# Cutting the feed-forward of an early-fusion layer into nine token tiles of 488 instead of eight batches of 548

## The chip, the cores and the metric

One core of a Trainium2 chip runs the whole kernel. TensorE (PE; its weight loads are PEld), VectorE (DVE), ScalarE (ACT) and GpSimd (POOL) compute; SyncE (SP) issues every DMA here. The metric is the time of one execution on the device, in microseconds (us), as the median over several runs. A profile is one execution, recorded instruction by instruction.

## The reference

Eight batches of 548 tokens (36 image patches, 512 text tokens) with 192 features pass through one layer. Only the last part is changed by this edit, the sum over 16 experts of a gelu network:

```python
h = h + attention(layernorm(h))            # h: (8, 548, 192)
xt = layernorm(h).reshape(-1, 192)         # 4384 tokens
comb = top8_softmax_weights(xt @ router_w.T)       # (4384, 16)
for e in range(16):                        # widths 8 x 128 and 8 x 256, 3072 in all
    hid = gelu(xt @ w1[:, off:off + wd])
    out = out + comb[:, e:e+1] * (hid @ w2[off:off + wd, :])
h = h + out
```

## The kernel before

**Phase A** runs attention, the second layer norm and the router, batch by batch. For each batch SP stores two things in DRAM: the normed input `x2` (three rows of 548 numbers for each of 128 partitions) and the weights `comb` (16 rows of 548). The sum `h` stays in SBUF, with 128 tokens to a partition block: `h[:, b, I, :]`. Phase A ends in a barrier of all engines (`end_of_phase_a`). SP reaches it only after `x2` of the last batch has landed in DRAM (line 236, waiting for `x2_stored`).

**The feed-forward** (lines 1031 to 1065 on DVE, 1085, 1441 and 1442 on PE) has the tokens as columns. For each batch it goes through 24 width tiles k of 128 rows of w1. Experts 0 to 7 have one tile each, experts 8 to 15 have two. Numbers are kept as a high and a low part, so each product costs several matmuls:

- `up(b, k)`: five matmuls for each half of 274 tokens, into two PSUM banks. Two pairs of banks alternate.
- ACT `gelu` writes `act`, DVE `weigh` multiplies it by `gate` (the row of `comb` for the expert, broadcast to 128 partitions), ACT `act_round` writes `act_hi`, DVE `act_rest` (line 795) writes `act_lo`.
- `down(b, k)`: five matmuls for each half, added up in banks 4 to 7 over all k.

PE issues `up(k + 2)` ahead of `down(k)`. On DVE `weigh(k + 1)` stands ahead of `act_rest(k)`, on ACT `gelu(k + 1)` ahead of `act_round(k)`. At the end of a batch ACT and DVE copy the sums out (`out_a`, `out_r`), PE transposes them back to tokens on partitions (ten transposes), DVE adds `h` (`h`, `out_t`), and SP stores the result. The next batch needs the same four banks, so its first `down` waits for that addition.

**What sets the order on SP.** Each engine works its own list in order. SP's list in the feed-forward is the loads of `gate` (four buffers; the load for expert e waits until expert e - 4 has been weighed), the stores of the output, and at one place the loads of `x2` for the last three batches. Those wait until POOL has split the rest of w2 (`w2_split`), since w2 is staged in the memory that they fill. Each load of `x2` also waits for the one before it to land. While SP waits at one instruction, nothing behind it is issued.

Of the kernel before, what the change touches and what calls it, by code (L numbers as in the profile page):

```python
# [31 lines left out]
P = 128  # L32
B = 8
# [31 lines left out]
CREDIT = 1  # L65

# [15 lines left out]
def early_fusion(nc, patches, txt, tok_w, tok_b, gammas, gn_w, gn_b, attn_w, w1, w2, out):  # L82
# [9 lines left out]
    with ctx:  # L92
# [75 lines left out]
        sb("x2_first", [P, B - 3, 3, L], F32, w2_staging)  # L168
        w2_others = sb("w2_others", [P, NW - W2_PART, 256], F32, w2_staging)
        w2_staging.close()  # L170
        x2_all = sb("x2_all", [P, B, 3, L], F32R)
        gate = [sb(f"gate{i}", [P, 2, HALF]) for i in range(4)]
        act = [sb(f"act{i}", [P, 2, HALF]) for i in range(3)]
        act_hi = [sb(f"act_hi{i}", [P, 2, HALF], F32R) for i in range(3)]
        act_lo = [sb(f"act_lo{i}", [P, 2, HALF], F32R) for i in range(3)]
        w2_hi, w2_lo = sb("w2_hi", [P, NW, P], F32R), sb("w2_lo", [P, NW, P], F32R)
        w2_r = sb("w2_r", [P, NW, P], F32R)
        out_a, out_r, out_t = sb("out_a", [P, L]), sb("out_r", [P, L]), sb("out_t", [P, NT, HD])
# [39 lines left out]
        outt_done, out_ready, out_stored = sem("outt_done"), sem("out_ready"), sem("out_stored")  # L218
# [25 lines left out]
        def _(sp):  # L244
# [27 lines left out]
            def store_x2(u, src):  # L272
                sp.wait_ge(x2_lo, nth(u, 3, 3))
                sp.dma_start(x2_dram[bass.ds(u, 1), :, :].rearrange("a p n -> p (a n)"),
                             src[:, :, :].rearrange("p c n -> p (c n)").bitcast(F32)).then_inc(x2_stored, 16)

            def store_ct(u):
                sp.wait_ge(ct_copied, CREDIT + nth(u, 1, 1))
                sp.dma_start(comb_dram[bass.ds(u, 1), :, :].rearrange("a e n -> e (a n)"),
                             ct[:, :]).then_inc(ct_stored, 16)  # L280

            def load_x2(b):
                if b:
                    sp.wait_ge(ld_x2, 16 * b)
                sp.dma_start(x2_all[:, b, :, :].bitcast(F32), x2_dram[b].rearrange("p (c n) -> p c n", c=3)).then_inc(ld_x2, 16)

            def body(b, tail, router, more):
                sp.wait_ge(w1_split, nth(b, 1, 1))
                if more:
                    sp.dma_start(w1_raw, w1[:, :, bass.ds((b + 1) * W1_SHARE, W1_SHARE)]).then_inc(ld_w1, 16)  # L290
                else:
                    sp.dma_start(w2_first, w2[:, 0:W2_PART, :]).then_inc(ld_w2, 16)
                if router:
                    store_x2(b - 2, x2)
                    store_ct(b - 2)

# [11 lines left out]
            for e in range(4):  # L308
                sp.dma_start(gate[e][:, :, :].rearrange("p a n -> p (a n)"),
                             comb_dram[0, e, :].partition_broadcast(P)).then_inc(ld_gate[e], 16)  # L310
            for b in range(2, B - 3):
# [8 lines left out]
            def gates(b, first, end=E):  # L320
                for e in range(first, end):

                    last = LAST_OF[(e - 4) % E] + 1
                    sp.wait_ge(gated, nth(b, NW, last) if e >= 4 else nth(b - 1, NW, last))
                    src = comb_dram[bass.ds(b, 1), e, :].rearrange("a n -> (a n)").partition_broadcast(P)
                    sp.dma_start(gate[e % 4][:, :, :].rearrange("p a n -> p (a n)"), src).then_inc(ld_gate[e % 4], 16)

            def store_out(b):
                sp.wait_ge(out_ready, nth(b, 2, 2))
                dst = out[bass.ds(b, 1), :, :].rearrange("a n d -> (a n) d")  # L330
                src = h[:, bass.ds(b, 1), :, :].rearrange("p a t d -> p (a t) d")
                sp.dma_start(dst[0:(NT - 1) * P, :].rearrange("(t p) d -> p t d", p=P), src[:, 0:NT - 1, :]).then_inc(out_stored, 16)
                sp.dma_start(dst[(NT - 1) * P:L, :], src[0:LAST, NT - 1, :]).then_inc(out_stored, 16)
# [11 lines left out]
            sp.wait_ge(out_stored, 32 * B)  # L345

# [108 lines left out]
        def _(sc_eng):  # L455
# [221 lines left out]
            def gelu(b, k):  # L677
                a.wait_ge(up_done, nth(b, NW, k + 1))
                if k >= 3 or not isinstance(b, int) or b:
                    a.wait_ge(act_lo_ready, nth(b, NW, k - 2))  # L680
                a.activation(act[k % 3][:, :, :], ps[:, 2 * (k % 2):2 * (k % 2) + 2, 0:HALF],  # L681
                             ACT.Gelu_apprx_tanh).then_inc(gelu_done, 1)

            def act_round(b, k):
                a.wait_ge(gated, nth(b, NW, k + 1))
                if k >= 3 or not isinstance(b, int) or b:
                    a.wait_ge(down_done, nth(b, NW, k - 2))
                copy(act_hi[k % 3][:, :, :], act[k % 3][:, :, :]).then_inc(act_hi_ready, 1)

            def ffn(b, more):  # L690

                gelu(b, 2)
                for k in range(2, NW - 1):
                    gelu(b, k + 1)
                    act_round(b, k)
                if more:
                    gelu(b + 1, 0)
                act_round(b, NW - 1)
                if more:
                    act_round(b + 1, 0)  # L700
                    gelu(b + 1, 1)
                a.wait_ge(down_done, nth(b, NW, NW))
                copy(out_a[:, :].rearrange("p (a n) -> p a n", a=2), ps[:, 4:6, 0:HALF]).then_inc(acc_a_copied, 1)
                if more:
                    act_round(b + 1, 1)

            gelu(0, 0)
            gelu(0, 1)
            round_w2(0, W2_HEAD)
            act_round(0, 0)  # L710
            act_round(0, 1)
            round_w2(W2_HEAD, W2_PART)
            ffn(0, True)
            with a.Fori(1, B - 1) as b:
                ffn(b, True)
            ffn(B - 1, False)


        @block.vector
        def _(dve):  # L720
# [306 lines left out]
            def weigh(b, k):  # L1027
                e = TILE_E[k]
                dve.wait_ge(gelu_done, nth(b, NW, k + 1))
                dve.wait_ge(ld_gate[e % 4], 16 * (b * (E // 4) + e // 4 + 1))  # L1030
                dve.tensor_tensor(act[k % 3][:, :, :], act[k % 3][:, :, :], gate[e % 4][:, :, :],  # L1031
                                  ALU.mult).then_inc(gated, 1)

            def act_rest(b, k):
                dve.wait_ge(act_hi_ready, nth(b, NW, k + 1))
                sub(act_lo[k % 3][:, :, :], act[k % 3][:, :, :], act_hi[k % 3][:, :, :]).then_inc(act_lo_ready, 1)

            def ffn(b, more):
                weigh(b, 2)
                for k in range(2, NW - 1):  # L1040
                    weigh(b, k + 1)
                    act_rest(b, k)
                if more:
                    weigh(b + 1, 0)
                act_rest(b, NW - 1)
                if more:
                    act_rest(b + 1, 0)
                dve.wait_ge(down_done, nth(b, NW, NW))
                dve.tensor_copy(out_r[:, :].rearrange("p (a n) -> p a n", a=2), ps[:, 6:8, 0:HALF]).then_inc(acc_r_copied, 1)  # L1049
                if more:  # L1050
                    weigh(b + 1, 1)
                dve.wait_ge(outt_done, nth(b, 1, 1))
                groups = []
                for r, t0, n, bank in ((P, 0, NT - 1, 4), (LAST, NT - 1, 1, 5)):
                    hb = h[:r, bass.ds(b, 1), t0:t0 + n, :].rearrange("p a t d -> p (a t) d")
                    main = ps[:r, bank, 0:P * n].rearrange("p (t d) -> p t d", t=n)
                    rest = ps[:r, bank + 2, 0:P * n].rearrange("p (t d) -> p t d", t=n)
                    groups.append((hb, rest, out_t[:r, t0:t0 + n, :]))
                    last = dve.tensor_tensor(hb[:, :, 0:P], main, hb[:, :, 0:P], ALU.add)
                last.then_inc(out_ready, 1)  # L1060
                for hb, rest, part in groups:
                    dve.tensor_tensor(part, rest[:, :, HD:P], hb[:, :, P:D], ALU.add)
                dve.drain()
                for hb, rest, part in groups:
# [438 lines left out]
```

## Time and profile before

| | |
|---|---|
| median of 3 runs | 899.78 us (898.18 to 900.14) |
| span of the profiled execution | 894.0 us, mean granted TensorE clock 0.969 |
| PE busy | 834.3 us, 93% of the span |
| DVE busy | 574.6 us, 64% |
| ACT busy | 495.9 us, 55% |
| POOL busy | 88.6 us, 10% |
| feed-forward | from the barrier at 377.9 us to the end |

The span runs from the first to the last instruction; what the runs add lies around it. A group of matmuls shows a mean duration that is longer than the distance between two starts, since they overlap; for the rate of a stream the starts are to be read.

### The profile page before, as it was taken

What the parts mean: (1) busy time and instruction counts of PE and PEld (TensorE: products, weight loads), DVE (VectorE), ACT (ScalarE), POOL (GpSimd) and SP (SyncE); (2) the same over time, 40 slices, a digit from 0 to 9 for tenths busy, and PEclk for the clock granted to TensorE, in tenths of its full rate; (3) what the DMA queues carried; (4) which work ended last, traced back from release to release, by engine and by line L of the source; (5) the groups of instructions that cost most, each with busy time, mean ns of one, the idle gap of its engine ahead of it and who ended that gap; (6) DMA issues with size and microseconds to landing.
All of it is one profiled execution on the core that took longest, in us unless ns stands there. A gap on an engine that the chain in (4) does not pass through costs nothing.

```text
span 894.0 us, 18035 instructions
## 1 busy us (share of the span) xinstructions
PE 834.3 (93%) x6048; PEld 764.7 (86%) x6048; DVE 574.6 (64%) x1574; ACT 495.9 (55%) x1102; POOL 88.6 (10%) x162
## 2 busy tenths in 40 slices
PE   5879999999999995779999999999999999999996
PEld 2757878797787874579999999999999999999996
DVE  6657788888888774685565555655655655655554
ACT  1467787887787785434444444444444444444443
POOL 3111131220203021160000000000000000000000
PEclk9789999999999997779999999999999999999999
DMA  8300010101101027422532232232322322322320
GB/s 237 118 19 18 1 57 2 55 2 57 50 7 55 2 75 271 155 76 64 172 104 73 64 95 75 63 90 80 75 75 81 88 63 78 103 71 63 94 65 20
DMA packets 34421, 67.30 MB, mean 75 GB/s; under 512 B 3632, under 2 KB 14160, under 8 KB 34256
## 3 DMA queue, kind: packets, MB, share of 16 engines
q1 hardware_dynamic: 34384, 66.84, 25.3%
q8 instruction: 20, 0.33, 0.1%
q14 instruction: 17, 0.14, 0.1%
HBM read 55.41 MB, written 11.42 MB: 75 GB/s over the span
## 4 chain that ended last, share of the span: by engine, by line
PE 73%; issue 14%; DVE 6%; POOL 2%; ACT 2%; POOLq 2%; DVEq 0%; PEldq 0%; ACTq 0%; PEld 0%
PE ps L1085 67%; PE ps L1224 3%; DVE sc L841 1%; ACT xn L472 1%; PE ps L1124 1%; DVE pr L864 1%; DVE x L795 1%; POOLq L379 1%; POOL w_lo L402 1%; DVE out_r L1049 1%; PE ps L1441 1%; PE ps L1442 0%; PE ps L1303 0%; DVE den L856 0%; DVE w_lo L795 0%
## 5 line engine op out<-in xcount | busy, mean ns | idle before, releaser
L1031 DVE TENSOR_TENSOR act<-act,gate 128x548 f32<-128x548 f32 x192 | 141.0, 738 | 202.8 <-ACT act L681 202.8
L681 ACT ACTIVATE act<-ps 128x548 f32<-128x548 f32 x192 | 120.5, 628 | 247.9 <-PE ps L1085 245.6
L1085 PE MATMUL ps<-x_all,w_hi 128*128 (+1 forms) x1152 | 252.9, 292 | 0.9 <-ACT act L681 0.9
L1085 PE MATMUL ps<-x_all,w_lo 128*128 (+1 forms) x768 | 216.4, 290 | 0.0
L1085 PEld LDWEIGHTS ps<-x_all,w_hi 128*128 128x128 f32 x1152 | 195.0, 190 | 1.2 <-PEq L236 1.0
L1085 PEld LDWEIGHTS ps<-x_all,w_lo 128*128 128x128 f32 x768 | 146.1, 190 | 0.0
L795 DVE TENSOR_TENSOR act_lo<-act,act_hi 128x548 fp32r<-128x548 f32 x192 | 141.6, 738 | 1.3
L459 ACT ACTIVATE act_hi<-act 128x548 fp32r<-128x548 f32 x192 | 125.7, 655 | 19.4 <-DVE act L1031 19.4
L1085 PE MATMUL ps<-act_hi,w_hi 128*128 128x274 f32 x384 | 112.7, 294 | 6.7 <-DVE act_lo L795 4.1
L1085 PE MATMUL ps<-act_lo,w_hi 128*128 128x274 f32 x384 | 111.6, 291 | 0.0
L1085 PE MATMUL ps<-act_hi,w_lo 128*128 128x274 f32 x384 | 111.6, 291 | 0.0
L1085 PE MATMUL ps<-act_lo,w_r 128*128 128x274 f32 x384 | 105.5, 291 | 0.0
L1085 PE MATMUL ps<-act_hi,w_r 128*128 128x274 f32 x384 | 105.1, 291 | 0.0
L1085 PE MATMUL ps<-pt,v 68*128 68x512 f32 (+5 forms) x288 | 82.9, 438 | 0.0
L1085 PEld LDWEIGHTS ps<-act_hi,w_hi 128*128 128x128 f32 x384 | 72.9, 190 | 7.6 <-DVE act_lo L795 4.6
L1085 PEld LDWEIGHTS ps<-pt,v 128*128 128x128 f32 (+1 forms) x288 | 49.3, 192 | 31.1 <-issue 21.7
L1085 PEld LDWEIGHTS ps<-act_hi,w_lo 128*128 128x128 f32 x384 | 73.3, 191 | 0.0
L1085 PEld LDWEIGHTS ps<-act_hi,w_r 128*128 128x128 f32 x384 | 73.2, 191 | 0.0
L1085 PEld LDWEIGHTS ps<-act_lo,w_hi 128*128 128x128 f32 x384 | 73.0, 190 | 0.0
L1085 PEld LDWEIGHTS ps<-act_lo,w_r 128*128 128x128 f32 x384 | 72.9, 190 | 0.0
L524 ACT ACTIVATE pr<-sc,nm 128x580 f32<-128x580 f32 (+4 forms) x120 | 67.2, 564 | 2.7 <-DVE nm L847 2.7
L1224 PE MATMUL ps<-ident,pr 128*128 128x128 f32 (+1 forms) x360 | 54.8, 282 | 11.3 <-DVE pr L864 8.0
(189 smaller groups left out, 1309.3 us busy)
## 6 DMA issues: line engine op xcount, KB each, us to landing
gate<-comb_dram SPq DMA_DIRECT2D x128, 274.0 KB, 3.3
x_all<-x_dram SPq DMA_DIRECT2D x8, 822.0 KB, 5.0
x_dram<-x SPq DMA_DIRECT2D x7, 822.0 KB, 3.4
w_raw<-w SPq DMA_DIRECT2D x8, 384.0 KB, 3.6
out<-h SPq DMA_DIRECT2D x8, 384.0 KB
w_others<-w SPq DMA_DIRECT2D x1, 2304.0 KB, 10.4
h<-txt SPq DMA_DIRECT2D x3, 672.0 KB
decay_rows<-drow SPq DMA_DIRECT2D x1, 1014.0 KB, 8.6
```

Of the source, the lines that this page charges most:

```text
L379: pool.drain()
L402: last = pool.tensor_tensor(w1_lo[:, c, cols], w1_raw[:, c, :], w1_hi[:, c, cols], ALU.subtract)
L459: return a.activation(dst, src, ACT.Copy)
L472: last = a.activation(dst[:r, I, 0:D], tokens(h, b, I), ACT.Identity, bias=nmean[:r, I:I + 1], scale=rs[:r, I:I + 1])
L524: last = a.activation(pr[s][:r, cols], sc[s][:r, cols], ACT.Exp, bias=nm[s][:r, I:I + 1], accum_out=row_sum[s][:r, I:I + 1])
L681: a.activation(act[k % 3][:, :, :], ps[:, 2 * (k % 2):2 * (k % 2) + 2, 0:HALF], ACT.Gelu_apprx_tanh).then_inc(gelu_done, 1)
L795: return dve.tensor_tensor(dst, src, hi, ALU.subtract)
L841: dve.tensor_tensor_reduce(out=dst, in0=src, in1=tab, scale=1.0 / 8, scalar=0.0 if I else NEG, op0=ALU.mult, op1=ALU.max, accum_out=mx[s][ ...
L864: last = dve.tensor_scalar(t, t, inv_den[s][:rows(I), I:I + 1], None, ALU.mult)
L1031: dve.tensor_tensor(act[k % 3][:, :, :], act[k % 3][:, :, :], gate[e % 4][:, :, :], ALU.mult).then_inc(gated, 1)
L1085: return pe.matmul(dst, w, x, start=start, stop=stop)
L1224: return pe.transpose(dst, pr[s][:r, at:at + n], ident[:r, :r])
```

## The change

The feed-forward no longer goes by batch. The 4384 tokens are one row, cut into nine tiles: eight of 488 and one of 480 (`width(t)`). A tile fits one PSUM bank (512 numbers), so there are no halves: `up(j)` and `down(j)` are five matmuls each, for 9 x 24 = 216 units j. `up` goes round four banks, the sums alternate between banks 4, 5 and banks 6, 7, and copying out, transposing and adding are moved into the units of the next tile: the copies behind unit 0, the eight transposes behind unit 1, the addition behind unit 3. Since tiles cross batches, `x2` and `comb` are laid out by token in DRAM, and `h` is stored in DRAM in phase A (`store_h`) and loaded again for each tile as four segments of 122 rows (`load_res`); the output is stored from the same form (`store_out`). The loops over batches are written out.

```diff
+TOKENS = B * L
+TW = 488
+NTT = -(-TOKENS // TW)
+SEG = 4
+X2_EARLY = 5
+def width(t):
+    return min(TW, TOKENS - t * TW)
...
-        x2_dram = nc.dram_tensor("x2_dram", [B, P, 3 * L], F32).ap()
-        comb_dram = nc.dram_tensor("comb_dram", [B, E, L], F32).ap()
+        x2_dram = nc.dram_tensor("x2_dram", [P, 3, TOKENS], F32).ap()
+        comb_dram = nc.dram_tensor("comb_dram", [E, TOKENS], F32).ap()
+        h_dram = nc.dram_tensor("h_dram", [TOKENS, D], F32).ap()
...
             store_x2(B - 2, x2)
             store_ct(B - 2)
+            store_h(B - 2)
             store_x2(B - 1, y)
+            store_h(B - 1)
             sp.wait_ge(x2_stored, CREDIT + 16 * B)
             end_of_phase_a(sp)
...
+            def by_segment(ap, t):
+                return ap[t * TW:t * TW + width(t), :].rearrange("(g p) d -> p g d", g=SEG)
+            def load_res(t):
+                if t >= 2:
+                    sp.wait_ge(out_stored[t % 2], 16 * (t // 2))
+                r = width(t) // SEG
+                sp.dma_start(res[t % 2][:r, :, :], by_segment(h_dram, t)).then_inc(ld_res, 16)
+            def store_out(t):
+                sp.wait_ge(out_ready, t + 1)
+                r = width(t) // SEG
+                sp.dma_start(by_segment(out_rows, t), res[t % 2][:r, :, :]).then_inc(out_stored[t % 2], 16)
             store_ct(B - 1)
-            gates(0, 4)
+            gates(0, 4, E // 2)
             sp.wait_ge(ct_stored, CREDIT + 16 * B)
             sp.wait_ge(w2_split, NW // W2_PART - 1)
-            for b in range(B - 3, B):
-                load_x2(b)
-            with sp.Fori(1, B) as b:
-                gates(b, 0)
-                store_out(b - 1)
-            store_out(B - 1)
+            for t in range(X2_EARLY, NTT):
+                load_x2(t)
+            sp.wait_ge(h_stored, 32 * B)
+            load_res(0)
+            gates(0, E // 2, E)
+            for t in range(1, NTT):
+                gates(t, 0, E // 2)
+                store_out(t - 1)
+                gates(t, E // 2, E)
+                sp.wait_ge(ld_res, 16 * t)
+                load_res(t)
+            store_out(NTT - 1)
...
+            def add_out(t):
+                r, bank = width(t) // SEG, 4 + 2 * (t % 2)
+                hb = res[t % 2]
+                main = ps[:r, bank, :].rearrange("p (g d) -> p g d", g=SEG)
+                rest = ps[:r, bank + 1, :].rearrange("p (g d) -> p g d", g=SEG)
+                dve.wait_ge(outt_done, t + 1)
+                dve.wait_ge(ld_res, 16 * (t + 1))
+                dve.tensor_tensor(out_t[:r, :, :], rest[:, :, HD:P], hb[:r, :, P:D], ALU.add)
+                dve.tensor_tensor(hb[:r, :, 0:P], main, hb[:r, :, 0:P], ALU.add)
+                dve.drain()
+                dve.tensor_tensor(hb[:r, :, P:D], rest[:, :, 0:HD], out_t[:r, :, :], ALU.add).then_inc(out_ready, 1)
...
+            for j in range(2, NTT * NW):
+                if j + 1 < NTT * NW:
+                    weigh(j + 1)
+                act_rest(j)
+                if j % NW == 0:
+                    acc_copy(j // NW - 1)
+                if j % NW == 3 and j > NW:
+                    add_out(j // NW - 1)
...
+            for j in range(NTT * NW):
+                if j + 2 < NTT * NW:
+                    up(j + 2)
+                down(j)
+                if j % NW == 1 and j > NW:
+                    out_transpose(j // NW - 1)
+            out_transpose(NTT - 1)
```

**Where instructions stand now.** The first place is SP's list from the last stores of phase A on. Before (`comb_dram<-ct` is `store_ct`, `x_dram<-` is `store_x2`, `x_all<-` is `load_x2`), the twelve gate loads of the first batch stand ahead of the three loads of `x2`:

```order
L274 DMA x_dram<-x 128x1644
L279 DMA comb_dram<-ct 16x548
L274 DMA x_dram<-y 128x1644
L279 DMA comb_dram<-ct 16x548
L326 DMA gate<-comb_dram 128x548 x12
L285 DMA x_all<-x_dram 128x1644 x3
```

In the changed kernel the same stretch, and the list of the next tile behind it:

```order
L292 DMA comb_dram<-ct 16x548
L298 DMA h_dram<-h 128x4x192
L299 DMA h_dram<-h 36x192
L288 DMA x_dram<-y 384x1x548
L298 DMA h_dram<-h 128x4x192
L299 DMA h_dram<-h 36x192
L292 DMA comb_dram<-ct 16x548
L349 DMA gate<-comb_dram 128x488 x4
L305 DMA x_all<-x_dram 128x3x488 x3
L305 DMA x_all<-x_dram 128x3x480
L359 DMA h<-h_dram 122x4x192
L349 DMA gate<-comb_dram 128x488 x16
```

Only four gate loads (experts 4 to 7) are left ahead of the loads of `x2`, which are now four, and the load of the residual stands there too; the gates of experts 8 to 15 come behind. At the barrier two stores of `h` now stand ahead of the last store of `x2`.

The second place is SP's list in a later tile of the changed kernel. The store of the output stands behind the gate of expert 7 and ahead of the gate of expert 8, and before the change it stood behind all sixteen gates of a batch:

```order
L364 DMA out<-h 122x4x192
L349 DMA gate<-comb_dram 128x488 x8
L359 DMA h<-h_dram 122x4x192
```

The third place is DVE's list at the addition of a tile in the changed kernel (`L1065` is `weigh`, `L828` is `act_rest`, the three rows in the middle are `add_out`):

```order
L1065 TENSOR_TENSOR act<-act,gate 128x488
L828 TENSOR_TENSOR act_lo<-act,act_hi 128x488
L1086 TENSOR_TENSOR out_t<-ps,h 122x256
L1087 TENSOR_TENSOR h<-ps,h 122x4x128
L1089 TENSOR_TENSOR h<-ps,out_t 122x4x64
L1065 TENSOR_TENSOR act<-act,gate 128x488
```

The addition now stands between `act_rest` of unit 3 and `weigh` of unit 5 of the next tile, where it stood at the turn from one batch to the next.

## Rows read from the trace of the kernel before

**Rows 1.** Waits from 440 us to the end: us in total, times, longest.

```profile
ACT act L681 <- PE ps L1085: 218.7, 170, 1.9
DVE act L1031 <- ACT act L681: 178.5, 149, 1.9
```

**Rows 2.** The chain around one turn of batches: start, us, what.

```profile
639.69 60.42 PE ps L1085 x475
...
701.31 0.11 PE ps L1442
...
702.29 60.46 PE ps L1085 x475
```

**Rows 3.** PE timeline in phase A: matmuls of 274, 420 and 292 columns.

```profile
328.67 0.35 PE L1085 MATMUL ps<-k_hi,q 128*128 128x420 f32 x1
328.86 0.35 PE L1085 MATMUL ps<-k_lo,q 128*128 128x420 f32 x1
329.05 0.30 PE L1085 MATMUL ps<-k_hi,q 128*128 128x292 f32 x1
```

**Rows 4.** Timelines of PE, ACT and DVE in one unit: start, us, what.

```profile
600.35 0.29 PE L1085 MATMUL ps<-x_all,w_lo 128*128 x1
...
600.68 0.63 ACT L681 ACTIVATE act<-ps 128x548 f32<-128x548 f32 x1 [1.36 <-PE ps L1085]
...
601.34 0.73 DVE L1031 TENSOR_TENSOR act<-act,gate 128x548 f32<-128x548 f32 x1 [1.17 <-ACT act L681]
601.99 0.72 DVE L795 TENSOR_TENSOR act_lo<-act,act_hi 128x548 fp32r<-128x548 f32 x1
...
603.01 0.29 PE L1085 MATMUL ps<-act_hi,w_hi 128*128 128x274 f32 x1
```

**Rows 5.** Groups by shape, DVE and ACT: busy us, mean ns of one.

```profile
L1049 DVE COPY out_r<-ps 128x548 f32<-128x548 f32 x8 | 5.8, 728 | 7.9 <-PE ps L1085 7.9
L1059 DVE TENSOR_TENSOR h<-ps,h 128x512 f32 x6 | 4.1, 691 | 5.6 <-PE ps L1442 5.6
L1062 DVE TENSOR_TENSOR out_t<-ps,h 128x256 f32<-128x256 f32 x8 | 3.2, 406 | 0.0
...
L681 ACT ACTIVATE act<-ps 128x548 f32<-128x548 f32 x192 | 120.5, 628 | 247.9 <-PE ps L1085 245.6 <-DVE act_lo L795 1.7 <-PEq L236 0.6
L459 ACT ACTIVATE pt<-ps 128x512 f32<-128x512 f32 x24 | 14.1, 586 | 17.8 <-PE ps L1224 17.7
```

**Rows 6.** SP at the barrier: its issue, and its wait.

```profile
374.33 0.42 SPq L274 DMA_DIRECT2D x_dram<-y  x1
...
SPq L236 <- DMA x_dram<-y: 3.1, 1, 3.1
```

**Rows 7.** Stretches at the start of the feed-forward: busy times, PEclk, DMA share, GB/s.

```profile
382.00:384.00 2.00, 0.00 (x0) 0.00 (x0) 2.00 (x3) 1.14 (x3) 2.00 (x3) 1.00 0.56 151
...
390.00:392.00 2.00, 2.00 (x10) 2.00 (x10) 2.00 (x3) 0.66 (x1) 1.85 (x3) 0.50 0.05 15
...
396.00:398.00 2.00, 2.00 (x18) 2.00 (x17) 0.66 (x2) 0.27 (x1) 0.00 (x0) 1.00 0.42 94
```

**Rows 8.** POOL's last piece of w2, and DVE's weigh of unit 4.

```profile
393.73 1.48 POOL L450 TENSOR_TENSOR w_r<-w_others,w_r 128x384 fp32r<-128x384 f32 x1
...
395.30 0.73 DVE L1031 TENSOR_TENSOR act<-act,gate 128x548 f32<-128x548 f32 x1 [0.94 <-ACT act L681]
```

**Rows 9.** DMA: issues to landing (page), and two loads of x2 on SP.

```profile
gate<-comb_dram SPq DMA_DIRECT2D x128, 274.0 KB, 3.3
x_all<-x_dram SPq DMA_DIRECT2D x8, 822.0 KB, 5.0
...
431.16 0.33 SPq L285 DMA_DIRECT2D x_all<-x_dram  x1
...
435.62 0.33 SPq L285 DMA_DIRECT2D x_all<-x_dram  x1
```

**Rows 10.** Stretches with a 92-row load, and with the last 128-row store.

```profile
12.50:13.00 0.50, 0.50 (x2) 0.09 (x2) 0.00 (x0) 0.00 (x0) 0.00 (x0) 1.00 0.28 91
13.00:13.50 0.50, 0.50 (x3) 0.30 (x2) 0.00 (x0) 0.36 (x1) 0.00 (x0) 1.00 0.27 92
...
892.00:892.50 0.50, 0.00 (x0) 0.00 (x0) 0.00 (x0) 0.00 (x0) 0.00 (x0) 0.50 1.00 323
```

**Rows 11.** SP's issues behind the 92-row load of h.

```profile
6.44 0.33 SPq L247 DMA_DIRECT2D h<-txt  x1
6.81 6.33 SPq L250 DMA_DIRECT2D h<-txt  x1
```

More of the change, by code:

```diff
@@ L315, in _, with gates @@
             store_x2(B - 1, y)
+            store_h(B - 1)
             sp.wait_ge(x2_stored, CREDIT + 16 * B)
             end_of_phase_a(sp)
-            def gates(b, first, end=E):
+            def gates(t, first, end):
+                n = width(t)
                 for e in range(first, end):
                     last = LAST_OF[(e - 4) % E] + 1
-                    sp.wait_ge(gated, nth(b, NW, last) if e >= 4 else nth(b - 1, NW, last))
-                    src = comb_dram[bass.ds(b, 1), e, :].rearrange("a n -> (a n)").partition_broadcast(P)
-                    sp.dma_start(gate[e % 4][:, :, :].rearrange("p a n -> p (a n)"), src).then_inc(ld_gate[e % 4], 16)
@@ L328, in store_out @@
[L328 to L333, printed above, removed]
+                    sp.wait_ge(gated, nth(t, NW, last) if e >= 4 else nth(t - 1, NW, last))
@@ L344, in _ @@
-            store_out(B - 1)
-            sp.wait_ge(out_stored, 32 * B)
+            for t in range(X2_EARLY, NTT):
+                load_x2(t)
+            sp.wait_ge(h_stored, 32 * B)
[8 more added lines that the diff above has]
+            store_out(NTT - 1)
+            for i in range(2):
+                sp.wait_ge(out_stored[i], 16 * (NTT // 2 + (NTT % 2 if i == 0 else 0)))
@@ L690, in ffn @@
[L690 to L705, printed above, removed]
@@ L1025, in w2_rest @@
                 sub(w2_r[:, k0:k1, HD:P], w2_first[:, k0:k1, P + HD:256], w2_r[:, k0:k1, HD:P]).then_inc(w2_lo_ready, 1)
[L1027 to L1062, printed above, removed]
-                dve.drain()
-                for hb, rest, part in groups:
-                    last = dve.tensor_tensor(hb[:, :, P:D], rest[:, :, 0:HD], part, ALU.add)
-                last.then_inc(out_ready, 1)
-                if more:
-                    act_rest(b + 1, 1)
@@ L1070, in _, with weigh, act_rest @@
-            weigh(0, 0)
-            weigh(0, 1)
+            def weigh(j):
+                t, e = j // NW, TILE_E[j % NW]
+                n = width(t)
+                dve.wait_ge(gelu_done, j + 1)
+                dve.wait_ge(ld_gate[e % 4], 16 * (t * (E // 4) + e // 4 + 1))
+                dve.tensor_tensor(act[j % 3][:, 0:n], act[j % 3][:, 0:n], gate[e % 4][:, 0:n], ALU.mult).then_inc(gated, 1)
+            def act_rest(j):
+                n = width(j // NW)
+                dve.wait_ge(act_hi_ready, j + 1)
+                sub(act_lo[j % 3][:, 0:n], act[j % 3][:, 0:n], act_hi[j % 3][:, 0:n]).then_inc(act_lo_ready, 1)
@@ L1072, in _ @@
+            weigh(0)
+            weigh(1)
             w2_rest(0, 0, W2_HEAD)
-            act_rest(0, 0)
-            act_rest(0, 1)
+            act_rest(0)
+            act_rest(1)
             w2_rest(1, W2_HEAD, W2_PART)
-            ffn(0, True)
-            with dve.Fori(1, B - 1) as b:
-                ffn(b, True)
-            ffn(B - 1, False)
+            weigh(2)
+            for j in range(2, NTT * NW):
+                if j + 1 < NTT * NW:
+                    weigh(j + 1)
+                act_rest(j)
+                if j % NW == 0:
+                    acc_copy(j // NW - 1)
+                if j % NW == 3 and j > NW:
+                    add_out(j // NW - 1)
@@ L1082, in _ @@
+            acc_copy(NTT - 1)
+            add_out(NTT - 1)
         @block.tensor
@@ L1409, in down @@
                     pe.wait_ge(w2_split, k // W2_PART)
+                if t >= 2 and k == 0:
+                    pe.wait_ge(out_ready, t - 1)
                 first, last_k = k == 0, k == NW - 1
-                hi, lo = act_hi[k % 3], act_lo[k % 3]
-                if k == 0 and (not isinstance(b, int) or b):
-                    pe.wait_ge(out_ready, nth(b - 1, 2, 1))
-                for n in range(2):
-                    mm(ps[:, 4 + n, 0:HALF], w2_hi[:, k, :], hi[:, n, :], first, False)
-                    mm(ps[:, 4 + n, 0:HALF], w2_lo[:, k, :], hi[:, n, :], False, False)
-                    mm(ps[:, 4 + n, 0:HALF], w2_hi[:, k, :], lo[:, n, :], False, last_k)
@@ new lines, in down, with out_transpose @@
+                mm(ps[:, bank + 1, 0:n], w2_r[:, k, :], lo, False, last_k).then_inc(down_done, 1)
+            def out_transpose(t):
+                r, bank = width(t) // SEG, 4 + 2 * (t % 2)
+                pe.wait_ge(acc_a_copied, t + 1)
+                pe.wait_ge(acc_r_copied, t + 1)
+                for g in range(SEG):
+                    pe.transpose(ps[:r, bank, g * P:(g + 1) * P], out_a[:, g * r:(g + 1) * r], ident[:, :])
+                    last = pe.transpose(ps[:r, bank + 1, g * P:(g + 1) * P], out_r[:, g * r:(g + 1) * r], ident[:, :])
+                last.then_inc(outt_done, 1)
```

175 lines of the change are left out of this document (86 added, 89 removed).

## The prediction

> **What bounds the kernel now.** I read the shares of busy time first (PE 93%), and then, since a mean hides stages, the waits of the feed-forward: ACT waits for PE 218.7 us in all, DVE for ACT 178.5 us, and nobody waits for anything else of that size [rows 1]. So PE sets the time from 440 us on. The chain of waits shows the same: 475 matmuls of 274 columns in 60.42 us, 127 ns each, then copies and ten transposes, then the next 475; from one batch to the next 62.6 us [rows 2]. A batch has 480 matmuls, 61.0 us, so a turn costs 1.6 us. A timeline of one unit shows how much room the other engines leave: the last matmul of `up` starts at 600.35, `act_lo` is ready at 602.71, the first `down` that reads it starts at 603.01 [rows 4]. Who feeds the gates (SP and the DMA queue) is seen nowhere as a bound, and that is where I look hardest below.
>
> **The change, part by part.**
>
> *Matmuls.* The columns are the same; 3840 matmuls of 274 become 1920 of 488 and 240 of 480. What counts is what 488 columns cost, and no row has them. The nearest have 420: starts 0.19 us apart [rows 3]. From 274 at 127 ns to 420 at 190.5 ns the slope is 0.436 ns a column, so I take 220 ns for 488 and 217 ns for 480. Ends: 226 ns, if cost goes by columns alone from 127 ns; 218.8 ns, if above 420 only 2.4 GHz counts. When `down` of unit 2 starts (about 395 us in both), 70 matmuls are done before and 35 after. Left are 3770 x 0.127 = 478.8 us, against 1885 x 0.220 + 240 x 0.217 = 466.8 us: **-12.0 us** (between +0 and -14).
>
> The Trainium skill, in "TensorE: Matmul & The Clock Gate", section "Wait — 56ns, not 53.3ns?", says that a warm matmul starts N/2.4 GHz plus about 2.5 ns after the last one. Row and rule differ here: 274 columns would be 116.7 ns by it, and the rows have 127. By the rule fewer instructions would save only 1645 x 2.5 ns, an estimate of 4.1 us.
>
> *Turns.* Seven turns of 1.6 us go (-11.2). Each of eight new ones has eight transposes of 0.11 us [rows 2] on PE, 0.9. The additions also delay DVE: 0.41 + 0.69 + 0.41 and a drain, 1.6 us [rows 5], stand between `act_rest` and the next `weigh`, where a unit of 10 x 0.22 = 2.2 us leaves DVE idle for 0.9. That makes 0.6 us late for the next `down`. Eight times 1.5: +12.0. Together **+0.8 us**.
>
> *The room of the other engines.* From the last `up` matmul to the ready `act_lo` it was 2.36 us of 2.66 [rows 4]. 60 columns fewer save about 1 ns each on ACT and DVE (628 against 586 ns and 728 against 691 ns for 36 columns [rows 5]), three times 0.06 us, and the longer matmul ends 0.09 us later: 2.27 us. The room is now 11 x 0.22 = 2.42 us, and a weight load must fit in too. I cost this at nothing; if it is 0.1 us short in each unit, half of that is lost 216 times: +11.
>
> *Barrier.* The last store of `x2` is issued at 374.33 and SP then waits 3.1 us for it [rows 6], which holds all engines. Two stores of `h` now stand ahead of it: two issues of about 0.35 us and 411 KB at 323 GB/s [rows 10], 1.3 us, partly overlapped. +1.4. The first units run on DVE beside POOL's split of w2, and five shorter operations give back 0.7; the tail has two transposes, some columns and a DMA issue less, -0.7. **0.0 us**.
>
> So without SP's list the span would be 894.0 - 12.0 + 0.8 = 882.8 us.
>
> *SP's list at the first tile.* POOL ends its last piece of w2 at 395.2 [rows 8], now about 396.6. Then come four loads of `x2`, each issued when the last has landed: 4.5 us from issue to issue [rows 9], so the fourth is issued at 410.3, the residual right behind, the gate of expert 8 at 411.1. DVE's `weigh` of unit 4 ran at 395.3 [rows 8]; with 0.5 for the shift and four units of 2.2 the weigh of unit 8 is due at 404.6. Behind it on DVE stands `act_rest` of unit 7, for which PE waits. With 3.3 us for the gate [rows 9] and 2 us for what lies ahead of it in the queue it would land at 416.4: 11.8 us late.
>
> *How fast a transfer of 122 rows is.* The residual and the output of a tile are 122 partitions x 3 KB, 375 KB. While a load of 92 rows was what the queue worked on, it moved 91 GB/s at a DMA share of 0.27; the last store, of 128 rows, moved 323 GB/s at a share of 1.00 [rows 10]. 0.27 of 16 engines is four, about 23 GB/s each (the store: 20). Four is the largest number up to 16 that divides 92; for 128 it is 16. By that reading 122 = 2 x 61 rows go over two engines: 375 KB at 40 to 46 GB/s are 8.2 to 9.3 us, where 16 engines take 1.2. And what is queued behind on those two engines waits: behind the 92-row load one issue held SP for 6.33 us [rows 11].
>
> The Trainium skill states this rule: "DMA: Bandwidth & Descriptors", section "Why a DMA increments its semaphore by 16 and not by 1", says that a DMA uses the largest number of engines up to 16 that divides its slowest dimension on both sides, with 100 partitions on ten and 127 on one. The trace agrees with its 0.27 for 92 rows.
>
> So the first gate also waits for the residual: two engines work on it from about 414.3 to 422.5, the gate lands at 423.2, **+18.6 us**.
>
> *SP's list in each later tile.* Let E be the end of `act_rest` of unit 3. The addition ends at E + 1.6, the store is issued at E + 1.7 and the gate of expert 8 right behind. Unit 5 is weighed at E + 1.6, unit 8 at E + 8.2. The gate lands after 1.7 + 8.7 (store) + 3.3 (gate) less about 1 us of overlapped start-up: E + 12.7 to 13.7. That is 4.5 to 5.5 us late. Ends: 3.2, if the store is at its fastest and the overlap larger; 7, if SP is held as behind the 92 rows. I take 4.8, near the plain sum, eight times: **+38.4 us**. The load of the residual is issued at unit 16 and the next gate is wanted at unit 24, 17 us later: it hides.
>
> *Clock.* When PE had idled through 382 to 384 its granted clock fell from 1.00 (2.4 GHz) to 0.50 (1.2 GHz) and was still there at 390 to 392 though PE was busy, and 1.00 again at 396 [rows 7]. Half speed for some 5 us costs 2.4 us. Nine stalls of 4 us and more: I take 2.0 each, **+18 us** (0 to 22).
>
> Sum: 882.8 + 18.6 + 38.4 + 18 = 957.8 us of span. The runs shown have a median 5.8 us above the profiled span (899.8 against 894.0), so **963.6 us**, 7% slower.
>
> **The rivals.**
>
> 1. *Transfers of 122 rows are as fast as those of 128.* For it: the DMA queue is only a quarter busy; against: 91 against 323 GB/s [rows 10]. The store then takes 1.2 us, the gate lands at E + 5.2 to 6.2, in time, and the point from which it decides is a store of 3.2 us. Left is the first stall: 882.8 + 11.8 + 2 = 896.6, a run of 902.4.
> 2. *Faster: gates are never late.* That needs rival 1, and that the four loads of `x2` cost SP under 4.7 us (404.6 - 3.3 - 396.6). The rows have 4.5 for each. If instead they overlap or land by half, and 488 columns cost 219 ns: 881 us, a run of 887, up to 897 with a short first stall.
> 3. *SP is held by the two slow engines.* Each issue behind a 122-row transfer waits as in [rows 11]: 7 us or more a tile and the next gates late too. 882.8 + 22 + 8 x 9 + 20 = 997, a run of 1003.
> 4. *DVE and ACT become the bound* (room 0.1 us short): +11 on the forecast, 975. By columns alone (226 ns): +12, much the same. And by the 2.5 ns rule, the Trainium skill's as above, the estimate would be some 8 us above my sum, inside the range.
>
> **How the numbers follow.** The forecast with rival 4 inside it: 0.72; rival 1: 0.11; rival 2: 0.07; rival 3: 0.10. The likeliest case's own range is 938 to 988: stalls of 3.2 to 6.5 us a tile are -13 to +14, the clock -16 to +4, matmuls and room -2 to +12. To leave out no more than 2 in 10 beside rivals 1 and 2, I give 928 to 992. Faster by over 0.2% (about what a measurement of this kernel can tell from no change) is rival 2, and a little of 1: 0.08; within 0.2%: 0.05; slower: 0.87.
>
> **What would show it.** *Matmuls*: starts of 488 columns 220 ns apart in an undisturbed unit, and units of 2.2 us. *Gates*: DVE idle ahead of `weigh` and put down to the DMA of `gate`, once for 12 to 19 us near 405 us, then once a tile for 4 to 6 us; in those stretches a DMA share near 0.12 and some 45 GB/s. *Clock*: 0.50 behind each stall. *Barrier*: SP's wait for `x_dram<-y` ends near 379.3. The forecast is wrong if the DMA share behind `out<-h` is near 1 (rival 1), or if SP's issues last several us each (rival 3).

## The result, and the profile after

The changed kernel takes **964.77 us** (median of 4 runs, 961.66 to 965.73). The kernel before took 899.20 us beside it (4 runs, 898.18 to 900.14). The ratio is 1.0724 (95% interval 1.0699 to 1.0749): 7.2% slower, where 963.6 us were forecast.

| | before | after |
|---|---|---|
| span of the profiled execution | 894.0 us | 963.9 us |
| mean granted TensorE clock | 0.969 | 0.930 |
| last `comb` store issued (just behind the barrier) | 378.00 us | 383.79 us |
| from there to the end | 516.0 us | 580.1 us |

The changed kernel's page: shares of busy time, the granted clock in 40 slices, and two DMA issues (count, KB each, median us to landing).

```profile
PE 851.8 (88%) x4360; PEld 685.6 (71%) x4360; DVE 576.0 (60%) x1602; ACT 500.9 (52%) x1151; POOL 88.1 (9%) x162
...
PEclk9789999999999966869989899899998998989989
...
gate<-comb_dram SPq DMA_DIRECT2D x128, 244.0 KB, 3.3
x_all<-x_dram SPq DMA_DIRECT2D x8, 732.0 KB, 4.5
```

From the 18th slice on (some 410 us) the clock is no longer an even row of nines: it dips about once in two and a half slices, some 61 us, which is one token tile. The median of a gate load is the 3.3 us of before [rows 9]. A median doesn't show the nine gates that matter. The waits from 395 us to the end do:

```profile
ACT act L720 <- PE ps L1113: 287.2, 213, 6.1
DVE act L1065 <- ACT act L720: 212.4, 185, 4.0
...
DVE act L1065 <- DMA gate<-comb_dram: 64.0, 9, 19.0
PE ps L1113 <- DVE act_lo L828: 55.5, 11, 17.8
```

In [rows 1] DVE waited for ACT and ACT for PE, and nobody for anything else of size. Now DVE waits 64.0 us for `gate`, nine times, and PE 55.5 us for what DVE then makes. The chain of waits gives the places, first tile and second:

```profile
400.51 4.51 DMA x_all<-x_dram
405.04 4.35 DMA x_all<-x_dram
409.40 4.49 DMA x_all<-x_dram
413.91 0.54 SPq L305
414.50 0.47 SPq L359
415.01 12.37 DMA gate<-comb_dram
427.47 0.10 DVE act L1065
...
477.70 10.99 DMA gate<-comb_dram
...
489.37 0.67 DVE act_lo L828
490.09 43.38 PE ps L1113 x185
```

Three of the four loads of `x2`, 4.4 to 4.5 us each, then the residual (L359), then a gate that takes 12.37 us to land. In the second tile the store of the output is issued at 477.37 and the gate of expert 8 right behind it, which takes 10.99 us; in the tiles after it 10.7. SP's own issue of these two gates is what takes long; SP's timeline, and the DMA share in the windows' columns of [rows 7] as the two issues end:

```profile
415.01 7.11 SPq L349 DMA_DIRECT2D gate<-comb_dram  x1
477.70 5.93 SPq L349 DMA_DIRECT2D gate<-comb_dram  x1
...
423.00:424.00 1.00, 0.00 (x0) 0.00 (x0) 0.00 (x0) 0.00 (x0) 0.00 (x0) 0.50 0.72 215
484.00:485.00 1.00, 1.00 (x6) 0.86 (x5) 0.00 (x0) 0.35 (x1) 0.00 (x0) 1.00 0.67 174
```

The issue behind the residual is held until 422.12, that behind the store until 483.63 (5.70 to 5.98 us in the eight tiles), where the median issue of a gate takes 0.33. `act_lo` of the unit that waited ends at 489.37 + 0.67, and seven tiles on at 918.77 + 0.66: 61.34 us a tile. What the DMA engines and PE do meanwhile:

```profile
480.00:482.00 2.00, 2.00 (x11) 1.71 (x10) 0.67 (x2) 0.94 (x2) 0.00 (x0) 1.00 0.13 39
482.00:484.00 2.00, 2.00 (x11) 1.64 (x10) 0.91 (x2) 0.86 (x3) 0.00 (x0) 1.00 0.14 47
...
486.00:488.00 2.00, 0.00 (x0) 0.00 (x0) 0.00 (x0) 0.06 (x1) 0.00 (x0) 0.96 0.81 133
...
490.00:495.00 5.00, 4.91 (x13) 4.07 (x14) 1.18 (x3) 0.54 (x2) 0.00 (x0) 0.53 0.22 54
495.00:500.00 5.00, 5.00 (x24) 4.18 (x23) 2.76 (x5) 2.59 (x6) 0.00 (x0) 1.00 0.09 32
```

While the store of 122 rows is worked on, the DMA share is 0.13 to 0.14 and 39 to 47 GB/s move: two engines of 16 (0.125). PE stands still from 485.5 on, its clock falls to 0.50 (1.2 GHz), and in the first five microseconds after the stall it starts 13 matmuls, where it starts 24 in the next five. The timeline shows both levels, first behind the stall, then in the middle of the tile:

```profile
490.66 0.61 PE L1113 MATMUL ps<-act_hi,w_lo 128*128 128x488 f32 x1
491.06 0.61 PE L1113 MATMUL ps<-act_lo,w_hi 128*128 128x488 f32 x1
...
510.23 0.39 PE L1113 MATMUL ps<-act_hi,w_lo 128*128 128x488 f32 x1
510.45 0.39 PE L1113 MATMUL ps<-act_lo,w_hi 128*128 128x488 f32 x1
```

Starts are 0.40 us apart at 0.50 and 0.22 us at 1.00.

### The profile page after: what moved, and what is told of

It reads as the page before. It is cut to its first block, busy times and chain, and to the rows that moved or that the text cites. A ratio compares the mean times of both kernels' runs of the same rounds, so it can differ in the third digit from the quotient of the medians.

```text
span 963.9 us, 13916 instructions
## 1 busy us (share of the span) xinstructions
PE 851.8 (88%) x4360; PEld 685.6 (71%) x4360; DVE 576.0 (60%) x1602; ACT 500.9 (52%) x1151; POOL 88.1 (9%) x162
## 4 chain that ended last, share of the span: by engine, by line
PE 58%; issue 16%; DMA 12%; DVE 6%; POOL 3%; ACT 2%; POOLq 2%; DVEq 1%; SPq 0%; ACTq 0%
PE ps L1113 53%; DMA gate<-comb_dram 10%; PE ps L1252 3%; DMA x_all<-x_dram 1%; DVE act_lo L828 1%; DVE sc L874 1%; ACT xn L510 1%; DVE act L1065 1%; PE ps L1152 1%; DVE pr L897 1%; DVE x L828 1%; POOL w_lo L487 1%; POOLq L417 1%; POOL w_lo L440 1%; ACT act L720 1%
## 5 line engine op out<-in xcount | busy, mean ns | idle before, releaser
L1065 DVE TENSOR_TENSOR act<-act,gate 128x488 f32<-128x488 f32 (+1 forms) x216 | 146.4, 678 | 280.7 <-ACT act L720 216.7
L720 ACT ACTIVATE act<-ps 128x488 f32<-128x488 f32 (+1 forms) x216 | 124.6, 577 | 288.8 <-PE ps L1113 287.2
L1113 PE MATMUL ps<-x_all,w_hi 128*128 128x488 f32 (+1 forms) x648 | 221.8, 397 | 0.9 <-SPq L250 0.9
L1113 PE MATMUL ps<-x_all,w_lo 128*128 128x488 f32 (+1 forms) x432 | 170.9, 396 | 0.0
L497 ACT ACTIVATE act_hi<-act 128x488 fp32r<-128x488 f32 (+1 forms) x216 | 130.3, 603 | 43.7 <-DVE act L1065 43.7
L1113 PE MATMUL ps<-act_hi,w_hi 128*128 128x488 f32 (+1 forms) x216 | 90.5, 419 | 61.9 <-DVE act_lo L828 60.7
L828 DVE TENSOR_TENSOR act_lo<-act,act_hi 128x488 fp32r<-128x488 f32 (+1 forms) x216 | 145.1, 672 | 0.1
L1113 PE MATMUL ps<-act_hi,w_lo 128*128 128x488 f32 (+1 forms) x216 | 86.3, 400 | 0.0
L1113 PE MATMUL ps<-act_lo,w_hi 128*128 128x488 f32 (+1 forms) x216 | 85.4, 395 | 0.0
L1113 PE MATMUL ps<-act_lo,w_r 128*128 128x488 f32 (+1 forms) x216 | 85.1, 394 | 0.0
L1252 PE MATMUL ps<-ident,pr 128*128 128x128 f32 (+1 forms) x360 | 55.2, 284 | 11.2 <-DVE pr L897 7.9
```

Of the source, the lines that this page charges most:

```text
L497: return a.activation(dst, src, ACT.Copy)
L720: a.activation(act[j % 3][:, 0:n], ps[:, j % 4, 0:n], ACT.Gelu_apprx_tanh).then_inc(gelu_done, 1)
L828: return dve.tensor_tensor(dst, src, hi, ALU.subtract)
L1065: dve.tensor_tensor(act[j % 3][:, 0:n], act[j % 3][:, 0:n], gate[e % 4][:, 0:n], ALU.mult).then_inc(gated, 1)
L1113: return pe.matmul(dst, w, x, start=start, stop=stop)
L1252: return pe.transpose(dst, pr[s][:r, at:at + n], ident[:r, :r])
```

## The experiments

Ratios are to the kernel before on the same chip (899.1 us beside the first four, 899.3 beside the next four, 897.6 beside the last three). The theory: transfers of 122 rows run on two engines and make gates late, and SP's list decides which. The rivals: the stall stays where SP's order puts it whatever a transfer's rows are; or the time is lost in the matmuls and additions themselves.

**1. Cut the rows into 112 + 10.** 112 can be divided by 16; the 10 left are small. Residual and output both:

```diff
-                sp.dma_start(by_segment(out_rows, t), res[t % 2][:r, :, :]).then_inc(out_stored[t % 2], 16)
+                for p0, p1 in ((0, 112), (112, r)):
+                    sp.dma_start(by_segment(out_rows, t)[p0:p1], res[t % 2][p0:p1, :, :]).then_inc(out_stored[t % 2], 16)
```

> Each residual load and each output store of a tile goes as two DMAs, 112 rows and 10 rows, instead of one of 122; the order on SP stays. Theory (122 rows run on two of sixteen engines): 112 rows run on sixteen, the store takes about 1.5 us instead of 8 to 9, the gate of expert 8 is in time in the tiles 1 to 8, and their eight stalls of PE with the half clock behind them go, 7.4 us each. The first tile still waits for the four x2 loads, some 12 us. 900 to 906 us. Rival A (what costs is that a store and a load stand ahead of the gates on SP at all, whatever engines they use): 950 to 966 us.

Measured: 902.67 us, ratio 1.0045 (1.0028 to 1.0062). 62.1 of the 65.6 us are gone with one more DMA for each residual and each store, and SP's issue of the gate behind them takes 0.36 and 0.74 us. One wait for `gate` is left, in the first tile, and in later tiles PE hardly stops. The wait, the chain, and from PE's timeline the first `down` matmul of four units that follow one another:

```profile
DVE act L1067 <- DMA gate<-comb_dram: 13.1, 1, 13.1
...
470.81 47.94 PE ps L1115 x215
...
525.26 48.00 PE ps L1115 x215
...
522.78 0.39 PE L1115 MATMUL ps<-act_hi,w_hi 128*128 128x488 f32 x1
525.26 0.49 PE L1115 MATMUL ps<-act_hi,w_hi 128*128 128x488 f32 x1
527.57 0.39 PE L1115 MATMUL ps<-act_hi,w_hi 128*128 128x488 f32 x1
529.79 0.38 PE L1115 MATMUL ps<-act_hi,w_hi 128*128 128x488 f32 x1
```

A tile takes 525.26 - 470.81 = 54.45 us without a stall. A unit of ten matmuls takes 2.22 us, 222 ns each, in nearly all of the tile. The two units at the addition take 2.48 and 2.31, 0.35 us more in sum, and the eight transposes 0.87; 240 x 0.222 and these make 54.5. So a stall cost 61.34 - 54.45 = 6.9 us a tile.

**2. All sixteen gates of the first tile ahead of the loads of `x2`,** rows uncut:

```diff
-            gates(0, 4, E // 2)
+            gates(0, 4, E)
...
-            gates(0, E // 2, E)
```

> In tile 0 all twelve gate loads are issued ahead of the x2 loads and the residual, as in the kernel before; 122 rows stay. Theory: the stall of 19 us near 408 us goes and with it some 3 us of half clock, the eight later ones stay: 940 to 945 us, DVE still waiting eight times 5.6 us for the gate. Rival B (the first stall only moves to a later gate or to the x2 loads): 955 us or more.

Measured: 956.7 us, 1.0648 (1.0614 to 1.0682): only 8.1 us won where 20 to 25 were expected, which is the time of rival B. The first tile has no stall now, but SP reaches the next tile's gates late. SP's timeline:

```profile
425.12 14.80 SPq L305 DMA_DIRECT2D x_all<-x_dram  x4
439.96 0.47 SPq L359 DMA_DIRECT2D h<-h_dram  x1
```

The loads of `x2` start only when the last gates have free buffers, at 425, so the first gates of tile 1 are issued from 440.48 on, and they stand behind the residual with its two engines (SP's issue of the first is held 7.18 us). PE is idle for 9.0 us from 445.5 on. The stall moved, and shrank.

**3. Both.**

> Both edits, 112 + 10 rows and gates first. Theory: no wait of DVE for a gate is left, the clock stays at 1.00 from 400 us to the end, and the sum without SP's list holds, 882.8 us of span in the prediction: 881 to 890 us, faster than the kernel before. If the wider matmuls and the added turns brought nothing in themselves, it would be 895 to 900.

Measured: 895.62 us, 0.9955 (0.9939 to 0.9972). Better than either, but outside the expected 881 to 890 and inside the range named for wider matmuls that bring nothing. The trace puts the miss down to the reason seen in experiment 2 instead: one wait for `gate` of 4.6 us in tile 1, 3.4 us of it on PE, with 6.8 us at half clock that begin just before it ends. Experiments 5 and 7 test this. The row cut is worth 61.1 us here and 62.1 us without the new order, so the two causes add up.

**4. Cut the rows into 61 + 61** (with the order of experiment 2). 61 has no divisor but itself, so if the divisor sets the number of engines this must be slower than uncut, and if small transfers as such help, faster.

> Gates first as in e2, and the 122 rows as two DMAs of 61 rows each. Theory (as many engines as divide the rows, up to sixteen): 61 is prime, both halves run on one and the same engine, a store takes 17 us, and each tile's stall grows by 8 to 9 us, more if the residual also comes late: 1005 to 1040 us. Rival C (any row count that is no multiple of 16 goes at one slow rate, or each DMA gets engines of its own): the bytes are the same, so 930 to 945 us as in e2.

Measured: 1054.63 us, 1.1732 (1.1691 to 1.1772), slower than the uncut rows by 98 us and past the upper end of what was expected. Windows, and the waits:

```profile
478.00:480.00 2.00, 2.00 (x11) 1.62 (x10) 1.03 (x2) 0.86 (x3) 0.00 (x0) 1.00 0.07 23
482.00:484.00 2.00, 0.00 (x0) 0.00 (x0) 0.00 (x0) 0.20 (x1) 0.00 (x0) 1.00 0.07 23
...
DVE act L1066 <- DMA gate<-comb_dram: 146.3, 16, 17.9
```

One engine of 16 (0.06) works, at 23 GB/s. The residual becomes slow enough to make the next tile's first gate late as well, so there are 16 waits instead of 9, which I take for the reason that it came out beyond the range. The Trainium skill, "DMA: Bandwidth & Descriptors", section "Why a DMA increments its semaphore by 16 and not by 1", has a DMA use the largest number of engines up to 16 that divides the slowest dimension on both sides; the shares here (0.07 for 61 rows, 0.13 to 0.14 for 122, 1.00 for 128 [rows 10]) agree with it.

**5. Experiment 3, and one load of `x2` a tile** instead of four in a row:

```diff
-            for t in range(X2_EARLY, NTT):
-                load_x2(t)
+            load_x2(X2_EARLY)
...
                 load_res(t)
+                if X2_EARLY + t < NTT:
+                    load_x2(X2_EARLY + t)
```

> As e3 (112 + 10 rows, gates first), and the four late x2 loads no longer stand in one row: one behind the residual of tile 0, the others one behind each later residual. Theory (in e3 the gate of expert 0 of tile 1 is issued at 441.7 us behind 14.8 us of x2 loads, PE idles 3.4 us and runs 6.8 us at half clock behind it): 6 to 7 us less than e3, 888 to 890 us, the granted clock 1.00 from 395 us to the end. Rival D (the gate only waits behind the residual instead, or the x2 load in a later tile delays gates): 893 to 897 us.

Measured: 888.03 us, 0.9882 (0.9855 to 0.9908). One wait for `gate` of 1.1 us is left, in the first tile. The 76.7 us between this and the changed kernel came from edits to SP's transfers and their order alone.

**6. Barrier and additions** (on top of 5): `store_h(6)` ahead of `store_ct(6)`, `store_h(7)` behind the barrier, and the third addition one unit later, so that DVE isn't late.

```diff
-                    add_out(j // NW - 1)
+                    add_out(j // NW - 1, False)
+                if j % NW == 4 and j > NW:
+                    add_more(j // NW - 1)
```

> As e5, and two small terms of the sum taken out: the store of h for batch 6 stands ahead of the comb store that waits for the router, that for batch 7 behind the barrier (I costed these at 1.4 us); the last of the three additions of a tile is moved behind unit 4 (0.3 to 0.6 us for each of eight tiles). 2 to 6 us less than e5: 883 to 887 us. If neither lies on the path, the same as e5.

Measured: 893.08 us, 0.9945 (0.9926 to 0.9963), 5.1 us worse than experiment 5 where 2 to 6 less was expected. The barrier did give its 1.2 us: from one `comb` store to the next 4.50 us where it was 5.71. But the addition one unit later makes the store, and the gate of expert 8 behind it, one unit later too, and a tile takes 55.16 us where it took 54.52 (mean of six), 5 us over eight tiles. Waits, SP's timeline and chain:

```profile
DVE act L1067 <- DMA gate<-comb_dram: 16.2, 8, 2.9
...
376.24 0.34 SPq L292 DMA_DIRECT2D comb_dram<-ct  x1
...
380.74 0.32 SPq L292 DMA_DIRECT2D comb_dram<-ct  x1
...
511.80 4.83 DMA gate<-comb_dram
```

**7. `up` in two halves of 244 columns** (on top of 5): the same columns in 1080 more matmuls.

```diff
+                for c in (slice(0, n // 2), slice(n // 2, n)):
+                    last = series(ps[:, j % 4, c],
+                                  [(w1_hi[:, 0, w], x[0][:, c]), (w1_lo[:, 0, w], x[0][:, c]), ...
```

> As e5, but each matmul of up is cut into two of 244 columns in the same bank, 1080 matmuls more, nothing else changed. Theory (a matmul costs a part that does not go by columns, 0.22 us at 488 against 0.127 at 274): two of 244 cost 0.226 to 0.236 us, so 3 to 15 us more than e5. Rival E (cost goes by columns alone): the same as e5 within 1 us.

Measured: 893.19 us, 0.9934 (0.9909 to 0.9959): 5.2 us more than experiment 5 by the medians, 4.8 ns for each added matmul. Their intervals would allow 2 to 8 ns; the traces have 54.98 us a tile where it was 54.52 (mean of six), 3.9 ns. A wide matmul does save time, and little.

**8. Tiles of 512** (`TW = 512`, four segments of 128 rows, the last tile 288 wide), with the orders of 2 and 5 and no row cut:

> As e5 in SP's order, but without cutting rows: tiles of 512 tokens (four segments of 128 rows) and a last one of 288 (four of 72). Theory (row counts set the number of engines): stores and residual loads of 128 rows take under 2 us without being cut, no gate is late, and the matmuls cost about the same in sum (1920 of 0.2325 us and 240 of about 0.135): 885 to 890 us. If ACT and DVE cannot follow in the last, narrow tile, up to 10 us more.

Measured: 886.25 us, 0.9857 (0.983 to 0.9884). 128 rows need no cut: SP's issue of the gate behind the store takes 0.50 us. The columns and the number of matmuls (9 x 240) are those of experiment 5, and the 1.8 us less are not told apart from it by these runs.

**9. Leave 122 rows uncut and move the store** behind all gates of its tile, where it stood before the change (with the orders of 2 and 5):

```diff
-                gates(t, 0, E // 2)
+                gates(t, 0, E)
                 store_out(t - 1)
-                gates(t, E // 2, E)
+                gates(t, E, E)
```

> Rows stay 122 and uncut; gates first and x2 loads spread as in e5; the store of a tile is moved behind all sixteen gates of the next one, just ahead of the residual load. Theory: store and residual, 8 to 9 us each on the same two engines, end 17 to 19 us after unit 16, and the gates of the next tile are wanted 17 us after it: a wait of 0 to 4 us a tile is left, 890 to 925 us. Rival F (a DMA on two engines holds SP so long that its place does not matter): 940 us or more.

Measured: 910.39 us, 1.0144 (1.0117 to 1.0171), in the middle of what was expected: order alone hides most of a slow store, not all (experiment 5, with the rows cut and the store ahead of the gate of expert 8, is 22 us less). SP's timeline:

```profile
538.54 0.30 SPq L364 DMA_DIRECT2D out<-h  x1
538.93 6.27 SPq L359 DMA_DIRECT2D h<-h_dram  x1
545.25 7.82 SPq L305 DMA_DIRECT2D x_all<-x_dram  x1
```

With a slow store and a slow residual back to back, SP's issue of the residual is held 6.27 us and that of the load of `x2` 7.82 us, as in [rows 11] and as the gate is in the changed kernel, and the next tile's gates are late (seven waits, 23.3 us in all, the longest 5.3).

**10. Experiment 8 with the stores of `h` off the barrier.**

> e8 (tiles of 512) with the two stores of h moved away from the barrier as in e6, where the time from the comb store of batch 6 to that of batch 7 fell from 5.7 to 4.5 us: about 1.2 us less than e8, 885 us. If e6 lost its time there and not at the gates: 2 us or more above e8.

Measured: 884.56 us, 0.9854 (0.9833 to 0.9875). 1.7 us less than experiment 8 by the medians, but the ratios are alike: not told apart by these runs.

**11. Experiment 10, the third addition one unit later, and the store moved two gates further back** (behind that of expert 9), which is what experiment 6 lacked:

```diff
-                gates(t, 0, E // 2)
+                gates(t, 0, E // 2 + 2)
                 store_out(t - 1)
-                gates(t, E // 2, E)
+                gates(t, E // 2 + 2, E)
```

> e10, with the last addition of a tile behind unit 4 as in e6, and the store behind the gate of expert 9 instead of 7, so that it no longer holds a gate. Theory (what e6 lost was the gate of expert 8, issued one unit later behind the store): 0 to 3 us less than e10, 882 to 885 us, no wait of DVE for a gate. If the later addition itself costs: 888 us or more.

Measured: **880.77 us, 0.9809 (0.979 to 0.9829)**, the fastest of all, 1.9% faster than the kernel before and 1.2 us below the expected range. No wait for `gate` is left, and the chain runs on PE from tile to tile:

```profile
453.20 55.09 PE ps L1123 x240
...
509.17 55.09 PE ps L1123 x240
```

229.5 ns for 512 columns, and 55.97 us from tile to tile: the turn is 0.88 us, the eight transposes alone. In experiment 10 a tile took 56.39 us (mean of five), so what the later addition gives is 0.4 us a tile.

## Why the prediction was right, and where its sizes were off

The three steps that carried the sum held. **Two engines for 122 rows** was read from a 92-row load, and experiments 1 and 4 show it from both sides. **The gate of expert 8 is late once a tile** is the nine waits, at the forecast places. **The clock falls behind each stall** is the granted 0.50. What the gate waits for was not what the forecast had (below). The result is that near the forecast because errors of both signs met, which is luck, so each term with its measure:

| term | forecast | measured |
|---|---|---|
| matmul of 488 columns | 220 ns | 222 ns (experiment 1) |
| tile without a stall | 54.3 us (52.8 + 1.5) | 54.45 us |
| first gate late by | 18.6 us | DVE 19.0, PE 17.8 us |
| gate of expert 8 lands | E + 12.7 to 13.7 us | E + 12.8 us (475.91 to 488.69) |
| PE idle in each later tile | 4.8 us | 4.3 to 4.6 us |
| half clock behind it | 2.0 us | 2.5 us (6.9 - 4.4); by PE's starts 2.2 to 2.3 in tiles 1 and 2 |
| stores of `h` at the barrier | 1.4 us | 1.2 us (experiment 6); 1.6 us from `comb` store to `comb` store |
| barrier to end, against before | +62.4 us | +64.1 us |

- *What the gate waits for* is the step that failed in its mechanism. The sum has SP issue the gate at once and lets it wait in the queue for the store's 8.7 us, to land 3.3 us later. The trace has SP's issue of the gate itself held, 5.93 us behind the store and 7.11 us behind the residual, and the gate lands 5.1 to 5.3 us after that issue ends. Both ways give E + 12.8 or so; that they agree is luck. This is the mechanism of *rival 3*, and its sign, issues of several us, came true. Its 1003 us did not, because its price was made of later gates: the next two are issued at 483.67 and 484.14, and DVE waits for neither.
- *Matmuls.* The slope from 274 and 420 columns gave 220 ns, measured are 222. Over 2125 matmuls 2 ns are 4 us, so a third of the -12.0 was not there. The Trainium skill's rule ("TensorE: Matmul & The Clock Gate", section "Wait — 56ns, not 53.3ns?") would have 488 columns at 205.8 ns, an estimate; the trace has 222. Its other half, a small fixed cost of each matmul, is there, as 4 to 5 ns in experiment 7 where the Trainium skill's rule has 2.5.
- *Turns.* The additions were to make the next `down` 0.6 us late. It is 0.35 us (experiment 1), and with tiles of 512 experiment 11 takes it away. A turn is 1.2 us and not 1.5, which gave back over half of what the matmuls took.
- *Room of the other engines.* Costed at nothing, and right: beyond the nine gates DVE and ACT wait for PE and one another, and the tile without a stall is as long as its matmuls, its transposes and the 0.35 us. Rival 4 did not come about.
- *Rival 1* (122 rows as fast as 128) fell with the DMA share of 0.13. But its time, 902.4 us, is what experiment 1 gave, 902.67 us, since cutting the rows makes it true. *Rival 2* is experiment 5: forecast 887, measured 888.03 us, once its two conditions are made true by edits. Both hits are luck in part: the two forecasts hold the 5.8 us of the next point, and the median spans measured (900.9 and 886.3) are 4 and 5 us above those forecast (896.6 and 881).
- *From the span to the median* is the step that was wrong in kind. I added 5.8 us as what the runs add around a span. In 99 of 101 runs with both numbers the time is 1.7 to 1.9 us above its own span (2.1 and 2.3 in two of experiment 7). The other 4.0 us I put down to the profiled execution of before being a short one, at 894.0: 39 more executions of that kernel had spans of 893.4 to 899.1 us, with a median of 896.9. What differs is where in phase A the clock is at half. The changed kernel's profile has such a stretch under the attention of the last batch:

```profile
342.00:344.00 2.00, 2.00 (x5) 0.97 (x5) 0.00 (x0) 0.43 (x1) 0.00 (x0) 0.50 1.18 474
344.00:346.00 2.00, 2.00 (x4) 0.88 (x4) 0.00 (x0) 0.00 (x0) 0.00 (x0) 0.50 1.01 433
346.00:348.00 2.00, 2.00 (x6) 1.28 (x4) 0.00 (x0) 0.00 (x0) 0.00 (x0) 0.53 1.01 433
```

In the profile of before the same three stretches had 1.00, 1.00 and 0.92, and up to 340 us the two profiles agree within 0.12 us of PE's busy time in every 100. `comb` of the last batch but one was stored at 378.10 us against 373.94: 4.2 us of the 5.8 up to the last `comb` store. I put them down to the execution and not to the change, and that is not shown: the same store stands at 375.69 to 378.23 us in the traces of the eleven experiments, in none as early as in the one trace of before. (Experiment 1, with the same phase A, was at 1.00 in 342 to 348 but at half clock for longer between 40 and 60 us.) So the forecast 957.8 for the span met a 963.9 of which 4.2 is this; behind the barrier the change cost 1.7 us more than forecast. Whether the loads and stores of the changed phase A make such a stretch likelier I did not test.

So the 65.6 us are made of 62.1 for transfers of 122 rows (experiment 1), 14.6 for SP's list in the first two tiles (from experiment 1 to 5), less 11.2 that the new form wins against the old one once both are gone (experiment 5). Of these 11.2 the matmuls (-8), the turns (-11.2 + 8 x 1.22) and the barrier (+1.2) explain 8.2, and with the -0.7 at the start and the -0.7 at the tail that I had only estimated it is 9.6.

## What to carry to other kernels

Before a tile size is chosen for what fits a PSUM bank, look at the number of partitions that it gives its DMAs: 122 rows, 61 and 112 + 10 are the same bytes, and took 956.7, 1054.6 and 895.6 us in one and the same order. A transfer on two engines also held the next issue of its queue for some 6 us here. And where loads that others wait for share a queue with stores, ask of each store how long the next load has before it is wanted; a store made one unit later (experiment 6) cost 5 us through the gate behind it. To set a forecast from a span against a median, take the gap from a run whose time and span are both known.

## What the runs showed of the hardware

- SP's issue of a 122-row transfer takes 0.28 to 0.47 us, but the issue right behind it is held: 5.70 to 5.98 us behind the store, 7.11 us behind the residual (7.18 in experiment 2), 6.27 and 7.82 us with two of them back to back (experiment 9), 8.06 us behind 61 rows (experiment 4), and 6.33 us behind the 92-row load [rows 11]. Behind 112 + 10 rows it takes 0.36 to 0.74 us, behind 128 rows 0.50.
- A gate of 128 rows behind a 122-row store lands 10.7 to 11.0 us after its issue began, where the median is 3.3. The DMA share stays at 0.12 to 0.14 from 479 to 484 us and goes to 0.67 in the microsecond after, and SP's issue of the gate ends at 483.63; behind the residual it ends at 422.12, and the share goes from 0.14 to 0.23 and then 0.72. So the idle engines get none of the gate's work while its issue is held. What holds the issue no run shows.
- The granted clock fell to 0.50 shortly before PE's 4.6 us of idle time ended at 490.09, and was back at 1.00 from 494.7 on: 6.8 us, of which 4.6 us with work, and these cost 2.2 us. A stall of 4.4 us is one of 6.9.
